# A gated delta-rule layer with a mixture of experts on one Trainium2 core: VectorE's list of the delta phase put in another order

## The reference

```python
q, k, v = x @ Wq.T, x @ Wk.T, x @ Wv.T                   # x: 2 x 2048 x 256; 16 heads of 64
q, k, v = (causal_dwconv(y, w, b) for ...)               # 4 taps along time, one filter per channel
g, beta = log_sigmoid(x @ Wg.T), sigmoid(x @ Wb.T)
k = k / max(norm(k), 1e-12);  q = q * 64 ** -0.5
for each token t:                                        # one state S (64 x 64) per batch and head
    delta = outer(v_t, k_t) - outer(S k_t, k_t)
    S = exp(g_t) * S + beta_t * delta
    o_t = S q_t
x = layernorm(x + o @ Wo.T)
```

## Time and profile before

| what | value |
|---|---|
| median of the runs | 1846.63 us |
| the profiled execution | 1854.48 us, of which the span from first to last instruction is 1852.7 us |
| TensorE, matmul | 1576.1 us busy, 85% of the span |
| VectorE | 1201.7 us, 65% |
| ScalarE | 890.0 us, 48% |
| GpSimd | 863.5 us, 47% |
| delta phase | about 60 to 1200 us of the span |

### The profile page before, as it was taken

How to read it: one execution, slowest core, us unless ns; L and a number is a source line. 1 busy time by engine, 2 the same in 40 slices (tenths; PEclk the granted TensorE clock), 3 DMA queues, 4 the chain that set the end, 5 groups by cost and what they waited for, 6 DMA issues and landing times. The chain is left out here.

```text
span 1852.7 us, 73957 instructions
## 1 busy us (share of the span) xinstructions
PE 1576.1 (85%) x31244; PEld 1175.0 (63%) x31244; DVE 1201.7 (65%) x3061; ACT 890.0 (48%) x2282; POOL 863.5 (47%) x1070
## 2 busy tenths in 40 slices
PE   7478999999899999999999997667888985898990
PEld 6235666666666666666666665556777874787870
DVE  1388988888889889888888886234445553222224
ACT  1276767767767767667667664100011110133333
POOL 0034444443444444434444443116655665577775
PEclk9799999999999999999999998887889997999995
DMA  6235564565555655655656554274444420499757
GB/s 269 82 83 115 114 133 114 124 128 116 123 126 114 138 113 123 135 114 113 137 114 126 111 117 99 56 240 118 140 130 133 138 80 27 110 259 248 166 88 284
DMA packets 521402, 245.45 MB, mean 132 GB/s; under 512 B 423888, under 2 KB 485968, under 8 KB 520176
## 3 DMA queue, kind: packets, MB, share of 16 engines
q1 hardware_dynamic: 368976, 200.72, 41.2%
q10 hardware_dynamic: 133632, 20.98, 6.1%
q0 software_dynamic: 18464, 19.03, 5.8%
HBM read 169.29 MB, written 71.37 MB: 130 GB/s over the span
## 5 line engine op out<-in xcount | busy, mean ns | idle before, releaser
L375 PE MATMUL delta_p_j<-delta_xt,delta_w 128*128 128x512 f32 x768 | 387.7, 628 | 30.5 <-DMA delta_xt<-in_xt 17.5
L574 DVE SCALAR_TENSOR_TENSOR delta_kq<-delta_hist,cw,delta_kq 128x512 f32<-128x512 f32 x384 | 298.6, 778 | 30.7 <-ACT delta_kq L722 23.7
L1395 POOL DMA_INDIRECT slot_tokens<-mix_tokens,mix_slot x192 | 188.5, 982 | 115.5 <-DVE mix_slot L1266 59.8
L715 ACT ACTIVATE delta_hist<-delta_p_j 128x512 f32<-128x512 f32 x192 | 114.8, 598 | 240.6 <-PE delta_p_j L375 233.4
L375 PEld LDWEIGHTS delta_p_j<-delta_xt,delta_w 128*128 128x128 f32 x768 | 132.0, 192 | 146.3 <-issue 111.8
L888 POOL TENSOR_TENSOR delta_sd<-state,eg_end 128x256 f32<-128x256 f32 x128 | 104.4, 816 | 258.2 <-DVE state L654 258.2
L1074 PE MATMUL mix_p_y<-mix_wo,mix_ot 128*128 128x256 f32 x512 | 134.3, 407 | 33.3 <-issue 15.6
L863 POOL TENSOR_SCALAR delta_n<-delta_n 128x8 f32<-128x8 f32 x64 | 15.5, 242 | 287.3 <-DVE delta_n L605 287.3
L1165 PE MATMUL mix_p_h<-mix_wo,w 128*88 128x128 f32 x1024 | 126.2, 277 | 13.5 <-ACT mix_wo L1351 10.4
L588 DVE SCALAR_TENSOR_TENSOR delta_yv<-delta_hist,cw,delta_yv 128x512 f32<-128x512 f32 x128 | 132.1, 1032 | 8.2 <-ACT delta_yv L722 5.9
L1074 PEld LDWEIGHTS mix_p_y<-mix_wo,mix_ot 128*128 128x128 f32 x512 | 99.3, 202 | 58.3 <-issue 44.9
(11 more groups left out here) (148 smaller groups left out, 3607.5 us busy)
## 6 DMA issues: line engine op xcount, KB each, us to landing
delta_xd<-x_scratch SPq DMA_DIRECT2D x256, 128.0 KB
delta_w<-in_wqkv SPq DMA_DIRECT2D x64, 416.0 KB
w<-in_w SPq DMA_DIRECT2D x64, 352.0 KB
delta_eg<-eg_rows SPq DMA_DIRECT2D x128, 130.0 KB, 3.2
n_scratch<-delta_kkq ACTq DMA_DIRECT2D x128, 128.0 KB
ot<-delta_o SPq DMA_DIRECT2D x128, 128.0 KB
mix_ot<-ot SPq DMA_DIRECT2D x16, 1024.0 KB
w<-in_w SPq DMA_DIRECT2D x64, 176.0 KB
```

Source lines behind the costliest of these rows:

```text
L375: mm = pe.matmul(p_j[:, :], w[e][:, (ch * 3 + n) * 128:(ch * 3 + n) * 128 + 128], xt[m // 8 % 2][:, ch * 512:ch * 512 + 512], start=ch == ...
L574: ve.scalar_tensor_tensor(out, view(hist[e], i * 2 * 518 + tap, (259, 2), (1, 256)), cw[:, column:column + 1], out, ALU.mult, ALU.add).the ...
L715: ac.activation(view(hist[e], n * 518 + 3, (259, 2), (1, 256)), p_j[:, :], ACT.Copy)
L1395: po.indirect_dma_start(out=s.tok.ap(), out_offset=bass.IndirectOffsetOnAxis(ap=slot[i % 2][:, k:k + 1], axis=0), in_=tokens[:, i:i + 1], ...
```

## The change

Only the order of VectorE's list changes; no arithmetic is added or removed, and no other engine's list is touched.

- `conv_values` is split into its two taps. Tap 2 of macro m stays in slot m. In even slots it stands where both stood, behind `update` two and ahead of the second correction y2; in odd slots it stands behind y2 and ahead of the mask. Tap 1 moves into slot m + 1, behind `residual` one and ahead of the query taps.
- In odd slots the key taps 1 and 0 go ahead of `residual` two. In even slots they stay behind it.
- The 15 substitution rows are shared out anew: before 6 in the odd slot (0-1, 2-5) and 9 in the even slot (6-8, 9-10, 11-14); after 8 in the odd slot (0-1, 2-3, 4-7) and 7 in the even slot (8, 9-10, 11-12, 13-14). The last batch of either slot (4-7 and 13-14) stands behind `inverse_lengths` and the first correction y1 and ahead of `update` two; before, all rows stood ahead of `inverse_lengths`.

```diff
--- before.py
+++ after.py
@@ -574,19 +574,18 @@
                     ve.scalar_tensor_tensor(out, view(hist[e], i * 2 * 518 + tap, (259, 2), (1, 256)),
                                             cw[:, column:column + 1], out, ALU.mult, ALU.add).then_inc(done, 1)
 
-            def conv_values(m):
+            def conv_values(m, tap):
 
                 e = m % 2
                 out = view(yv[e], 0, (256, 2), (1, 256))
-                for tap in (2, 1):
-                    if tap == 2:
-                        ve.wait_ge(tap_v, m + 1)
-                        ve.wait_ge(carried, m + 1)
-                    else:
-                        ve.wait_ge(conv_v, 2 * m + 1)
-                    column = (m % NPAIR * 3 + 2) * (TAPS + 1) + tap
-                    ve.scalar_tensor_tensor(out, view(hist[e], 518 + tap, (259, 2), (1, 256)),
-                                            cw[:, column:column + 1], out, ALU.mult, ALU.add).then_inc(conv_v, 1)
+                if tap == 2:
+                    ve.wait_ge(tap_v, m + 1)
+                    ve.wait_ge(carried, m + 1)
+                else:
+                    ve.wait_ge(conv_v, 2 * m + 1)
+                column = (m % NPAIR * 3 + 2) * (TAPS + 1) + tap
+                ve.scalar_tensor_tensor(out, view(hist[e], 518 + tap, (259, 2), (1, 256)),
+                                        cw[:, column:column + 1], out, ALU.mult, ALU.add).then_inc(conv_v, 1)
 
             def gate(m):
                 e = m % 2
@@ -665,17 +664,18 @@
                 if one:
                     residual(*one)
                 if is_macro(before):
+                    conv_values(before, 1)
                     conv(before, 1, tap_q, conv_q)
                     gate(before)
                 if even:
-                    substitute(subst_group, range(6, 9))
+                    substitute(subst_group, range(8, 9))
                 if one:
                     update(*one)
                 if is_macro(m):
-                    conv(m, 0, tap_k, conv_k, (2,))
+                    conv(m, 0, tap_k, conv_k, (2, 1, 0) if t % 2 else (2,))
                 if two_:
                     residual(*two_)
-                if is_macro(m):
+                if is_macro(m) and t % 2 == 0:
                     conv(m, 0, tap_k, conv_k, (1, 0))
                 if even:
                     substitute(subst_group, range(9, 11))
@@ -684,19 +684,25 @@
                 if is_macro(before):
                     lengths(before)
                 if even:
-                    substitute(subst_group, range(11, SUB - 1))
+                    substitute(subst_group, range(11, 13))
                 if odd:
-                    substitute(subst_group, range(2, 6))
+                    substitute(subst_group, range(2, 4))
                 if is_macro(before):
                     inverse_lengths(before)
                 if is_macro(mi):
                     horner(mi, rx_done, 16, y1_out)
+                if even:
+                    substitute(subst_group, range(13, SUB - 1))
+                if odd:
+                    substitute(subst_group, range(4, 8))
                 if two_:
                     update(*two_)
-                if is_macro(m):
-                    conv_values(m)
+                if is_macro(m) and t % 2 == 0:
+                    conv_values(m, 2)
                 if is_macro(mi):
                     horner(mi, ry1_done, 32, y2_out)
+                if is_macro(m) and t % 2:
+                    conv_values(m, 2)
                 if is_macro(before):
                     mask(before)
```

## The result

The changed kernel took 1871.6 us (median of four runs, 1862.5 to 1878.5) beside 1846.4 us for the kernel before: a ratio of 1.0132, with a 95% interval of 1.0086 to 1.0178. The forecast was 1872 us. The profiled execution took 1873.18 us with a span of 1871.4; before it was 1854.48 and 1852.7.

A forecast was written before the change was run, and what follows sets the result against it. TensorE and VectorE, both full, alternately hold each other up; a pair of slots goes from 33.74 to 9.59 + 14.14 + 10.83 = 34.56 us, so 25 us over 29 pairs: 1872 us, range 1840 to 1890 (likeliest sign 1860 to 1890).

The forecast's parts named there:

- Term one: From `inverse_r` in the odd slot to the next even slot's first state product: 10.29 - 0.70 = 9.59 us.
- part 1: Value tap 1 into the next slot, odd tap 2 behind y2: frees TensorE's 0.70 us wait for y2; cover large.
- part 2: Key taps ahead of the odd residual, where VectorE idles 2.56 us: worth nothing on the path by itself.
- Term two: From the even slot's first state product to the inverse's transpose: 12.63 + 0.53 + 0.98 = 14.14 us.
- The block: Rows 13 and 14 in even slots held up by GpSimd's `weight`: bounded from 0 to 1.04 us, taken as 0.98.
- The near row: Value tap beside `weight` in the kernel before: took 1.35 us, ended 0.54 after `weight`; used to size the rows' delay.
- Parts 1 and 3: Tap 1 costs VectorE the same in the next slot; rows 6 and 7 leave even slots, residual stays at 7.54 us.
- The trip: From the transpose's start to `inverse_r` in the odd slot, nearly all DMA: 10.83 us, unchanged.
- The even slot's wait for y2: TensorE's idling for y2 in even slots: y2 some 0.35 us earlier, about half of the idle time kept.
- The `kb` rival: `kb` loads, behind the inverse's in SyncE's queue, come too late: another 0.6 us a pair, 1889 us; chance 0.17.
- The sum: Pair of slots 34.56 us against 33.74, 0.82 longer; over 29 pairs 24 us, taken as 25: 1872 us.
- The power of 8 columns: GpSimd's 2.11 us instruction from 632.87: second value tap finished by 634.16 regardless, disagreeing with the skill's exclusion rule.

The follow-up runs named there:

- even rows first: Changed kernel with rows 11 to 14 of even slots all ahead of the reciprocal and y1 again; ratio 0.9919 to the kernel before.
- reciprocal behind the rows: Changed kernel with the even slots' reciprocal moved behind rows 13 and 14 (y1, rows, reciprocal); 1841.7 us, ratio 0.9966 to the kernel before.
- the second execution: The changed kernel, unaltered, traced again on the chip of the follow-up series; ratio 1.0112 to the kernel before.

## Why the prediction was right, and where it was not

**Term one (9.59).** Measured 9.54 us in the pair shown, right in size there. Over all pairs the median fell by 0.30 (10.30 to 10.00) in the first traced execution and by 0.68 (10.31 to 9.63) in the second, where 0.70 was forecast; the pairs with TensorE at half clock are the long ones. Wrong in its reason: part 1 credited it to the value taps alone and called part 2 worth nothing. The key taps alone give 0.992 and clear the same wait. The step that failed is "worth nothing on the path by itself": I compared the residual's start, which does not move, and did not follow the list on to y2, where about 1.4 us less of work stands.

**Term two (14.14).** Measured 13.81 in the pair shown, 13.98 by the median. y1 and the reciprocal cost the 0.53 forecast: row 13 starts 0.53 us after the reciprocal (605.81 to 606.34). The block was sized at 0.98 and is 0.77 (0.96 instead of about 0.19). One instruction of the four ran ahead of `weight`, and I had counted too much for the three behind it; the prediction's own working gave 0.99 to 1.14 against the unblocked case, and 0.98 was taken. The other 0.12 us of the miss is the reciprocal, which came that much sooner than counted. The near row, the value tap that ended 0.54 us after release, was a poor guide to how fast a small instruction ends after release: 0.04.

**Parts 1 and 3, the residual stays at 7.54.** True for the two together, and the sum used them together. Taken alone each step was wrong: value tap 1 delays the residual by up to 0.9 us in the kernel with the old rows, and it is the departure of rows 6 and 7 that pays for it. Part 1's "the cover is large" looked only at who reads the tap's result, not at what queues behind the tap.

**The trip (10.83).** As a pattern it was long: the median is 10.1 before and 10.2 after, and the hidden ones take 9.4 after, which the trace of before could not show. So 17 odd slots wait for the load from 200 to 1150 us (18 of the 28 with the very short waits) and not nearly all, 1.26 us each by the mean and not 1.5 to 2.5. At equal trip the three terms give 0.43 us a pair (13.81 + 9.54 against 12.63 + 10.29), not 0.82.

**The even slot's wait for y2.** Forecast to be halved, it is gone: the block was 0.21 us shorter and the reciprocal came 0.12 sooner, which together is about what was forecast to remain.

**The `kb` rival.** It happened in part, as allowed for: 23 waits. Mostly they are covered; TensorE's wait for y2 is 3.1 us in all.

**What was missed:** ScalarE's query tap. It stands behind the transpose in ScalarE's list, so TensorE's next projection waits 0.7 us in 28 odd slots. Where the load is later still, it costs nothing. In the odd slots that do not wait for the load (10 of 28) it stands in TensorE's path, in place of the wait for y2 of the even slot that is gone; no run took it out, so its price is not shown.

**What was missed, and weighs more: TensorE's clock.** The prediction counts a wait at its own length. In the first traced execution the six longest waits for the load each came with a stretch at half clock, and up to 12 of the 16 us between the masks are that. The term is not in the sum.

**The sum.** 25 us forecast, 25.2 measured between the medians. The agreement is luck: the steady pairs gave 16 us and not 24 in the first traced execution and under 3 in the second, and of the 16 up to 12 are a clock term that the sum does not have. The first slots gave another 4.8, and the runs themselves spread by 16 us. What holds is the mechanism, the place and the sign. Two runs show that the place of the inverse's end costs more than the taps win (even rows first, reciprocal behind the rows), and two traces put the block at 0.75 to 0.77 us. How the 1.3% divides between the direct cost and the clock is an estimate from four traces; that the early slots' share is more than chance is not shown, as the second execution did not have it.

The rule of the Trainium skill ("SBUF — State Buffer", section "Who interferes with whom") held for `tensor_tensor` on VectorE against `tensor_tensor` on GpSimd: 0.96 us instead of 0.19. It says that any GpSimd instruction that reads SBUF contends; for one SBUF input the traces bear it out in part. Beside GpSimd's `tensor_scalar` of 64 columns an instruction took 0.26 us instead of 0.19, within single pieces of 0.44 us, which is less than a block to the end of the piece. But GpSimd's copy took 0.67 us instead of 0.19 beside VectorE's taps, which is a clash with a one-input instruction. The power of 8 columns, which the prediction took for a counterexample, need not be one: it took 2.11 us where a tap was running at its start and 1.66 where none was, so it was held up itself. (The tap that the prediction has finished by 634.16 ended at 634.24.)

## What to carry to other kernels

In an engine's hand-written list, cost a moved instruction by what stands behind it up to the next thing that another engine waits for, not by who reads its result; two edits that clear the same wait count once, and an edit that looks worthless may be the one that pays for another. When a long trip (here two DMAs, 10 us) starts from one place in a list, the place where it starts is what decides, and moving two small rows in front of the reciprocal turned 1.3% lost into 0.8% won. Before placing small two-input instructions, look at what GpSimd runs at that moment: one `tensor_tensor` there makes a 0.2 us instruction last 1 us. And look at the granted clock behind each long wait of TensorE before putting the whole loss down to the wait: here the stretches at half clock took up to 12 of 16 us in one execution, and up to 34 of 76 in another.

## What the runs showed of the hardware

- GpSimd's eight `tensor_scalar` of 64 columns took 3.4 to 4.0 us, its one `tensor_tensor` of 512 columns 1.04: short instructions cost it 0.4 to 0.5 us each.
- The power of 8 columns (L882 before, L888 after) takes 2.11 us if a two-input tap of VectorE is running when it starts, and 1.66 if none is, even where a tap starts later, as at 608.19 in the changed kernel. Its mean fell from 2093 to 1676 ns there, which is 27 of the 34 us by which GpSimd's busy time fell.
- TensorE's granted clock fell from 2.4 to 1.2 GHz for 3.41 us, or twice that, in 6 places of the changed kernel's delta phase between the two masks. Each came with a wait of TensorE of 1.6 to 2.35 us. Not every such wait has one: of the second execution's, one of 1.61 us has none.
- Chips differ by 4.8% on the same kernel (1762 against 1846 us), and mostly not in this phase: the last state product ends at 1201.6 us of 1852.7 in the kernel before, and at 1192 of 1756 with the value taps alone on a faster chip, so 87 us between these two executions lie in the routing and expert phase. Why is not settled here.
